# VectorE's products of a trace one piece ahead of its scans in a four-layer residual kernel

## What is computed

```python
ctx = causal_ema(x, tau_ctx)
wg = sigmoid(concat([x, ctx]) @ Wg.T + bg)
gated = x * wg
h1 = gelu(x @ Wn1.T + bn1)
mod = 0.5 + sigmoid(h1 @ Wn2.T + bn2)                 # one factor per token and trace
traces = [causal_ema(gated * mod[..., d], tau_raws[d]) for d in range(16)]
temporal = sum_d traces[d] * softmax(blend)[d]
gate = sigmoid(temporal @ Wtemp.T + btemp)
soma = gelu(x @ Wsoma.T + bsoma)
x = x + layernorm((soma * gate) @ Wout.T) * gamma + beta
x = x + pooled_attention(x)                           # second layer
x = x + mixture_of_9_experts(x)                       # third layer: 8 experts and a shared one
x = x + two_layer_head(x, expert_index)               # fourth layer
```

## Time and profile before

| | us |
|---|---|
| median of 3 runs (2808.72 to 2808.73) | 2808.72 |
| span of the profiled execution, first to last instruction | 2807.6 |
| TensorE busy | 2770.3 |
| VectorE busy | 1796.9 |
| ScalarE busy | 1449.7 |
| GpSimd busy | 1218.6 |
| mean granted TensorE clock | 0.998 |

### The profile page before, as it was taken

How to read it: one execution, slowest core, us unless ns; L and a number is a source line. 1 busy time by engine, 2 the same in 40 slices (tenths; PEclk the granted TensorE clock), 3 DMA queues, 4 the chain that set the end, 5 groups by cost and what they waited for, 6 DMA issues and landing times.

```text
span 2807.6 us, 36696 instructions
## 1 busy us (share of the span) xinstructions
PE 2770.3 (99%) x12794; PEld 2299.4 (82%) x12794; DVE 1796.9 (64%) x2976; ACT 1449.7 (52%) x2625; POOL 1218.6 (43%) x950
## 2 busy tenths in 40 slices
PE   8799999999999999999999999999999999999999
PEld 5678888888888888888888888888888888888888
DVE  8799778867777666556765766555766563333443
ACT  4555666566456544555545644455644563333445
POOL 5256435633554355434543345433454333333334
PEclk9999999999999999999999999999999999999999
DMA  4244333433223322112321222211322131111221
GB/s 154 81 145 125 100 105 104 145 98 102 77 68 99 107 68 68 57 59 69 104 64 59 82 87 74 68 47 57 111 80 66 42 103 45 46 45 46 79 89 58
DMA packets 117383, 230.37 MB, mean 82 GB/s; under 512 B 13672, under 2 KB 58960, under 8 KB 117200
## 3 DMA queue, kind: packets, MB, share of 16 engines
q1 hardware_dynamic: 81808, 190.15, 22.1%
q10 hardware_dynamic: 32832, 29.49, 4.2%
q0 software_dynamic: 2560, 8.39, 1.0%
HBM read 219.89 MB, written 8.09 MB: 81 GB/s over the span
## 4 chain that ended last, share of the span: by engine, by line
PE 93%; DVE 4%; issue 1%; ACT 1%; DMA 0%; SPq 0%; DVEq 0%; ACTq 0%
PE bank L588 20%; PE bank L589 20%; PE bank L590 20%; PE ps_out L588 10%; PE ps_out L590 10%; PE ps_out L589 10%; PE bank L581 1%; DVE trace L1130 1%; DVE trace L1138 1%; DVE w_lo L1210 1%; DVE hid L1244 0%; PE ps_out L581 0%; DMA pre_x<-in_xT 0%; PE bank L709 0%; PE bank L700 0%
## 5 line engine op out<-in xcount | busy, mean ns | idle before, releaser
L1383 POOL TENSOR_TENSOR hid_lo<-hid,hid_hi 128x512 fp32r<-128x512 f32 x640 | 851.0, 1330 | 1532.3 <-ACT hid_hi L1015 1532.0
L588 PE MATMUL bank<-res_lo,w_hi 128*128 128x512 f32 x2432 | 957.1, 394 | 5.7 <-DVE hid L1244 2.6
L589 PE MATMUL bank<-res_hi,w_lo 128*128 128x512 f32 x2432 | 948.6, 390 | 0.0
L590 PE MATMUL bank<-res_hi,w_hi 128*128 128x512 f32 x2432 | 947.4, 390 | 0.0
L1244 DVE TENSOR_TENSOR hid<-hid,bank 128x512 f32<-128x512 f32 x576 | 394.1, 684 | 623.5 <-PE bank L590 597.9
L984 ACT ACTIVATE hid<-bank 128x512 f32<-128x512 f32 x576 | 343.9, 597 | 589.0 <-PE bank L590 588.0
L1210 DVE TENSOR_TENSOR w_lo<-w_raw,w_hi 128x768 fp32r<-128x768 f32 (+2 forms) x520 | 495.0, 954 | 194.3 <-ACT w_hi L946 152.1
L946 ACT ACTIVATE w_hi<-w_raw 128x768 fp32r<-128x768 f32 x392 | 331.3, 845 | 480.5 <-PE ps_out L590 468.5
L588 PEld LDWEIGHTS bank<-res_lo,w_hi 128*128 128x128 f32 x2432 | 457.2, 188 | 99.0 <-issue 4.6
L590 PEld LDWEIGHTS bank<-res_hi,w_hi 128*128 128x128 f32 x2432 | 457.0, 188 | 96.9
L589 PEld LDWEIGHTS bank<-res_hi,w_lo 128*128 128x128 f32 x2432 | 457.4, 188 | 89.7
(11 more groups left out here) (180 smaller groups left out, 1565.4 us busy)
## 6 DMA issues: line engine op xcount, KB each, us to landing
w_raw<-in_chunks SPq DMA_DIRECT2D x392, 384.0 KB
mod_on<-mod_rows ACTq DMA_DIRECT2D x154, 128.0 KB
w_raw<-in_head_chunks SPq DMA_DIRECT2D x64, 224.0 KB
stat<-mod_rows ACTq DMA_DIRECT2D x70, 128.0 KB, 3.2
x_in<-in_xT SPq DMA_DIRECT2D x16, 256.0 KB, 3.8
pre_x<-in_xT SPq DMA_DIRECT2D x14, 256.0 KB, 7.3
soma_rows<-pre_soma SPq DMA_DIRECT2D x14, 256.0 KB, 2.0
soma<-soma_rows SPq DMA_DIRECT2D x14, 256.0 KB, 3.6
```

Of the source, the lines that this page charges most:

```text
L588: mm(out, wh, xl, start=start and i == 0, stop=False, skip_group_check=not lone)
L589: mm(out, wl, xh, start=False, stop=False, skip_group_check=not lone)
L590: last = mm(out, wh, xh, start=False, stop=end, skip_group_check=not lone)
L1383: nc.gpsimd.tensor_tensor(hid_lo[i % DEPTH][:], hid[i % 3][:], f(hid_hi[i % DEPTH][:]), ALU.subtract).then_inc(s_hlo, 1)
```

## The change

Piece 7 + d on VectorE now holds the product of trace d and then the scan of trace d-1; piece 7 holds only a product, and a new piece 23 only scan 15. GpSimd's addition of trace d moves from piece 8 + d to piece 9 + d; add 15 comes in piece 24, ahead of the gather. ScalarE's mix d waits for scan d-2 (mix 1: for mul 0) in place of scan d-1, which is the last VectorE work of the piece before in both versions. The product's wait for GpSimd begins at d = 3 in place of d = 4: mul 3 and mul 4 both wait for add 1, mul d for add d-3. The costs of pieces 7 and 23 change from 2.1 and 0.7 to 0.8 and 1.3, so the planner deals the pieces of blocks 1 to 7 anew.

```diff
--- before.py
+++ after.py
@@ -87,8 +87,8 @@
 
 def side_cost(b, j):
 
-    if 7 <= j < 7 + ND:
-        return 2.1
+    if 7 <= j <= 7 + ND:
+        return {7: 0.8, 7 + ND: 1.3}.get(j, 2.1)
     if b == 0 and j in (1, 26, 30, 32, 45):
         return 0.0
     return {0: 1.3, 5: 1.0, 34: 1.7, 36: 1.4, 42: 1.5, 24: 0.0, 25: 0.0, 29: 0.0, 37: 0.0, 43: 0.0}.get(j, 0.7)
@@ -267,7 +267,7 @@
 SIDE_ACT = (["x_hi", "ctx_hi", "h1", "soma", "mod", "gate", "alpha"] + [f"mix{d}" for d in range(ND)]
             + ["t_hi", "tgate", "p_hi", "sq", "q_hi", "cen", "std", "attn", "exp", "xT", "probT"])
 SIDE_DVE = (["ctx", "x_lo", "ctx_lo", "mod", "mod_hi", "modpair", "gated"]
-            + [f"{what}{d}" for d in range(ND) for what in ("mul", "scan")]
+            + [name for d in range(ND) for name in ([f"mul{d}", f"scan{d - 1}"] if d else ["mul0"])] + [f"scan{ND - 1}"]
             + ["t_lo", "prod", "p_lo", "q_lo", "rstd", "norm", "affine", "x1", "score",
                "max", "top", "xT_lo", "den", "rden", "prob", "probT_lo", "res"])
 SIDE_POOL = [f"add{d}" for d in range(1, ND)]
@@ -932,7 +932,7 @@
                     act.wait_ge(l_act[s], act_at(s, b, f"mix{d - 1}"))
                     if d + 2 < ND:
                         spread(s, b, d + 2)
-                    act.wait_ge(l_dve[s], dve_at(s, b, f"scan{d - 1}"))
+                    act.wait_ge(l_dve[s], dve_at(s, b, f"scan{d - 2}" if d > 1 else "mul0"))
                 act.wait_ge(s_on[s][k], 16 * ((ND // 3 + (k < ND % 3)) * (b - 1) + d // 3 + 1))
                 activate(ps_side[s][:, 0:S], mod_on[s][k][:], ACT.Copy, bias=1.0, scale=0.5).then_inc(l_act[s], 1)
 
@@ -1113,31 +1113,35 @@
                 elif j == 6:
                     dve.wait_ge(l_act[s], act_at(s, b, "gate"))
                     STT(gated[s][:], gated[s][:], 1.0, X[:], ALU.add, ALU.mult).then_inc(l_dve[s], 1)
-                elif 7 <= j < 7 + ND:
+                elif 7 <= j <= 7 + ND:
                     d = j - 7
-                    tr = trace[s][d % 3]
-                    if d == 0:
-                        mine("gated")
-                    if d == 0 and b == 0:
-                        done("blend")
-                    if d > 3:
-                        dve.wait_ge(l_pool[s], pool_at(s, b, f"add{d - 3}"))
-                    if b:
-                        dve.wait_ge(l_act[s], act_at(s, b, f"mix{d}"))
-                    else:
-                        dve.wait_ge(l_pe[s], pe_at(s, b, f"mix{d}"))
-                    for h in range(DH):
-                        last = STT(tr[:, h, :], gated[s][:, h, :], bl[:, h, d:d + 1],
-                                   (lead_mix[d % 2] if lead else ps)[:, 0:S], ALU.mult, ALU.mult)
-                    last.then_inc(l_dve[s], 1)
-                    mine(f"mul{d}")
-                    if d == 0 and b == 0:
-                        dve.wait_ge(l_act[0], act_at(0, b, "alpha"))
-                    decay = ps[:, S + d:S + d + 1] if b else lead_alpha[:, d:d + 1]
-                    for h in range(DH):
-                        last = V.tensor_tensor_scan((temporal[s] if d == 0 else tr)[:, h, :], decay.broadcast_to([P, S]),
-                                                    tr[:, h, :], 0.0, ALU.mult, ALU.add)
-                    last.then_inc(l_dve[s], 1)
+                    if d < ND:
+                        tr = trace[s][d % 3]
+                        if d == 0:
+                            mine("gated")
+                        if d == 0 and b == 0:
+                            done("blend")
+                        if d > 2:
+                            dve.wait_ge(l_pool[s], pool_at(s, b, f"add{max(d - 3, 1)}"))
+                        if b:
+                            dve.wait_ge(l_act[s], act_at(s, b, f"mix{d}"))
+                        else:
+                            dve.wait_ge(l_pe[s], pe_at(s, b, f"mix{d}"))
+                        for h in range(DH):
+                            last = STT(tr[:, h, :], gated[s][:, h, :], bl[:, h, d:d + 1],
+                                       (lead_mix[d % 2] if lead else ps)[:, 0:S], ALU.mult, ALU.mult)
+                        last.then_inc(l_dve[s], 1)
+                    if d:
+                        d -= 1
+                        tr = trace[s][d % 3]
+                        mine(f"mul{d}")
+                        if d == 0 and b == 0:
+                            dve.wait_ge(l_act[0], act_at(0, b, "alpha"))
+                        decay = ps[:, S + d:S + d + 1] if b else lead_alpha[:, d:d + 1]
+                        for h in range(DH):
+                            last = V.tensor_tensor_scan((temporal[s] if d == 0 else tr)[:, h, :], decay.broadcast_to([P, S]),
+                                                        tr[:, h, :], 0.0, ALU.mult, ALU.add)
+                        last.then_inc(l_dve[s], 1)
                 elif j == 26 and b:
                     dve.wait_ge(l_act[s], act_at(s, b, "t_hi"))
                     TT(one_lo[s][:], temporal[s][:], f(one_hi[s][:]), ALU.subtract).then_inc(l_dve[s], 1)
@@ -1362,7 +1366,7 @@
 
             def side(b, s, j):
                 if j == 24:
-
+                    add(b, s, ND - 1)
                     if b == 0:
                         done("onehot")
                     pool.wait_ge(l_pool[s], pool_at(s, b, f"add{ND - 1}"))
@@ -1370,13 +1374,15 @@
                     nc.gpsimd.indirect_dma_start(
                         out=trace[s][2][:].rearrange("p j l -> p (j l)"), out_offset=None, in_=penalties[:],
                         in_offset=bass.IndirectOffsetOnAxis(ap=pen_row[:, q:q + 1], axis=0)).then_inc(s_pen[s], 16)
-                elif 9 <= j < 8 + ND:
-                    d = j - 8
-                    pool.wait_ge(l_dve[s], dve_at(s, b, f"scan{d}"))
-                    if d > 1:
-                        pool.wait_ge(l_pool[s], pool_at(s, b, f"add{d - 1}"))
-                    nc.gpsimd.tensor_tensor(temporal[s][:], temporal[s][:], trace[s][d % 3][:],
-                                            ALU.add).then_inc(l_pool[s], 1)
+                elif 10 <= j < 9 + ND:
+                    add(b, s, j - 9)
+
+            def add(b, s, d):
+                pool.wait_ge(l_dve[s], dve_at(s, b, f"scan{d}"))
+                if d > 1:
+                    pool.wait_ge(l_pool[s], pool_at(s, b, f"add{d - 1}"))
+                nc.gpsimd.tensor_tensor(temporal[s][:], temporal[s][:], trace[s][d % 3][:],
+                                        ALU.add).then_inc(l_pool[s], 1)
 
             def late(i):
                 pool.wait_ge(s_hhi, i + 1)
```

## The result

The changed kernel takes **2831.96 us** (median of 4 runs, 2831.83 to 2833.25) against 2808.72 (4 runs, 2808.72 to 2812.88): ratio 1.0078, 95% interval 1.0066 to 1.0091. It is slower by 23 us, and the prediction, 2807.9 with a range up to 2816.0, missed it. The profiled execution took 2831.83 with a span of 2829.7; 2.1 us lie around the span, not 1.1 as I had assumed. The span grew by 22.1.

The account below looks back on a forecast made before the run. The prediction took TensorE, busy 99%, to bound the kernel. Lead -2.4, block 1's first lane +1.6 and the rest 0 summed to -0.8: span 2806.8, time 2807.9 us, range 2801.5 to 2816.

Parts of the forecast that it names:

- Base: Whole kernel: forecast summed on the profiled span of 2807.6 us, with 1.1 us added for the time around it.
- Lead, term 1: Block 0: scans no longer wait for the product just ahead, saving 0.12 us a trace over 29 pairs, -3.5 us.
- rival that the wait costs nothing: Block 0's traces: leaving out the wait gains nothing, so term 1 is 0 and the time 2811.4 us; chance 0.13.
- Lead, term 2: Block 0: product 3 newly waits for add 1 on GpSimd, starting at about 25.3 instead of 23.9 us, +1.4.
- the second wait: Block 0: a later product waits for GpSimd once, after lane 0's last addition and its penalty gather, 0.1 to 0.2 us.
- Block 1's first lane: 118 to 171 us: product 3's stall and more pieces before the next hids delay TensorE, +1.6 us, between 0 and +3.5.
- The rest: After 171 us: product 3's stalls are absorbed and TensorE's 12.0 us of idle stay, +-4, so 0 us.
- Product 3 reaching TensorE: Blocks after block 0: product 3's stalls delay TensorE, +10.3 us in all, time 2819.0; chance 0.15.
- That of no effect: Whole kernel: lead gain and lead stall cancel and block 1 is as before, time 2808.7 us; chance 0.08.
- The closings' idle: Closings of runs: shorter, newly dealt pieces remove half of TensorE's 12.0 us idle, time 2801.9 or 2800.3; chance 0.17.

Follow-up runs that it names:

- e9: e6 with each scan waiting for the product directly ahead of it instead of its own, same instructions and order: 2810.58 us.
- e2: The changed kernel with product 3 waiting for scan 0 on VectorE instead of add 1 on GpSimd: 2825.79 us.
- e1: The changed kernel with add 15 back in piece 23, the rest as changed: 2818.92 us.
- e7: The changed kernel with add 15 in piece 23 and product 3 waiting for scan 0, new costs kept: 2811.47 us.
- e5: The kernel before with the new order in block 0 only, product 3 not waiting for GpSimd, old costs: 2807.7 us.
- e6: The changed kernel with old costs, add 15 in piece 23 and product 3 waiting for scan 0: 2805.66 us.
- e8: The kernel before with only add 15 moved into piece 24, old order and old costs: 2818.36 us.
- e3: The kernel before with only the planner's new costs of pieces 7 and 23: 2818.26 us.

## Why the prediction was wrong, point by point

**Base.** Span plus 1.1 should have been span plus 2.1 for the changed kernel; that is 1 us of the 24 by which the forecast missed. (On the later chips the same difference is 1.8 for the kernel before.)

**Lead, term 1 (-3.5).** Right in cadence. VectorE in the changed kernel:

```profile
43.85 0.85 DVE L1131 SCALAR_TENSOR_TENSOR trace<-gated,bl,bank 128x256 f32<-128x256 f32 x2
44.62 1.26 DVE L1142 TENSOR_TENSOR_SCAN trace<-bank,trace 128x256 f32<-128x256 f32 x2
45.80 0.85 DVE L1131 SCALAR_TENSOR_TENSOR trace<-gated,bl,bank 128x256 f32<-128x256 f32 x2
```

1.95 us a trace, where the earlier trace rows had 2.07. The rival that the wait costs nothing is refuted for these two instructions by e9. The Trainium skill (VectorE: DVE Perf Modes, "The DRAIN you can't avoid") says that the flush is paid whether or not a semaphore follows and that the semaphore costs nothing extra; 2.07 against 1.94 us for the same instructions in the same order does not agree with that for this pair.

**Lead, term 2 (+1.4).** The wait is where and as long as forecast:

```profile
21.36 0.87 DVE L1131 SCALAR_TENSOR_TENSOR trace<-gated,bl,bank 128x256 f32<-128x256 f32 x2 [2.38 <-PE bank L661]
...
23.49 1.27 POOL L1384 TENSOR_TENSOR temporal<-temporal,trace 128x512 f32<-128x512 f32 x1 [2.32 <-DVE trace L1142]
24.80 0.87 DVE L1131 SCALAR_TENSOR_TENSOR trace<-gated,bl,bank 128x256 f32<-128x256 f32 x2 [1.39 <-POOL temporal L1384]
```

Its price was right too. From the third product's start to prod of lane 0 the changed kernel takes 63.84 us and e2, which lacks this wait alone, 62.51: 1.33. With add 15 early it is 64.23 in e1 and 62.93 in e7: 1.30. What was mis-sized is the second wait, forecast at 0.1 to 0.2 and 0.96 in the changed kernel:

```profile
79.14 0.87 DVE L1131 SCALAR_TENSOR_TENSOR trace<-gated,bl,bank 128x256 f32<-128x256 f32 x2 [0.96 <-POOL temporal L1384]
...
85.19 0.67 DVE L1152 SCALAR_TENSOR_TENSOR trace<-trace,soma 128x512 f32<-128x512 f32 x1
```

Lead in sum: prod 2.2 us earlier than in the earlier trace rows, the first hid 2.0, forecast 2.4. **Right**, with some luck: from the third product to prod VectorE gained only 1.8 (65.62 before, 63.84 now), and the third product itself came 0.4 earlier, which is scatter more than order: it starts at 21.46 to 22.08 in the three traces of the old order and at 21.03 to 21.93 in the nine of the new one. My own mark for it, the first expert matmul at 115.9 instead of 118.3, failed in this trace, 117.93, for another reason: TensorE's clock. It ran at its half level for longer behind the traces than in the kernel before; by 5 us (same columns as the windows above), the changed kernel:

```profile
101.00:106.00 5.00, 3.11 (x10) 2.01 (x10) 4.12 (x10) 2.67 (x7) 0.00 (x0) 0.65 0.14 33
106.00:111.00 5.00, 4.38 (x14) 3.70 (x15) 3.13 (x9) 2.06 (x6) 0.00 (x0) 0.50 0.41 128
...
116.00:121.00 5.00, 3.07 (x14) 2.57 (x15) 1.69 (x3) 2.04 (x4) 0.00 (x0) 1.00 0.00 0
```

and the kernel before:

```profile
106.00:111.00 5.00, 3.23 (x13) 2.41 (x14) 4.12 (x11) 4.10 (x12) 0.00 (x0) 0.79 0.27 81
...
116.00:121.00 5.00, 2.74 (x9) 2.21 (x9) 1.98 (x3) 1.10 (x3) 0.00 (x0) 0.81 0.00 0
```

0.50 is 1.2 GHz, 1.00 is 2.4 GHz; in the 5 us in which it fell TensorE was busy 3.11, in the 5 before (97.5 to 102.5) 2.91. Behind the first expert matmul the kernel before had its own slow stretch and the changed one had none, so by the first hid the gain was back. In e5, e6 and e7 that matmul came at 115.53, 115.75 and 115.92.

**Block 1's first lane (+1.6, between 0 and +3.5).** Right in size, in part by luck: -2.0 at the 1st hid, +0.1 at the 15th, +2.1. Product 3's stall, forecast at 4.7 us:

```profile
152.18 1.30 POOL L1384 TENSOR_TENSOR temporal<-temporal,trace 128x512 f32<-128x512 f32 x1
153.51 0.87 DVE L1131 SCALAR_TENSOR_TENSOR trace<-gated,bl,bank 128x256 f32<-128x256 f32 x2 [4.38 <-POOL temporal L1384]
...
163.81 0.60 PE L588 MATMUL bank<-res_lo,w_hi 128*128 128x512 f32 x1 [1.88 <-DVE hid L1248]
```

4.38 us. The addition ran 2.9 us earlier than I had placed it, and TensorE's wait came at 163.81, for hid, not at 171. In sum TensorE waited no longer between the two hids than before (1.9 and 0.6 us now; 0.7, 1.1 and 0.6 before). The clock is what differs. The changed kernel:

```profile
163.00:168.00 5.00, 4.20 (x12) 3.31 (x12) 5.00 (x8) 2.57 (x5) 3.67 (x3) 0.66 0.46 145
```

and the kernel before:

```profile
162.00:167.00 5.00, 3.86 (x17) 2.91 (x16) 5.00 (x5) 1.90 (x4) 2.83 (x3) 1.00 0.59 191
```

0.34 of 5 us is 1.7 us, most of the 2.1, and the prediction had no such term. The wait of product 3 is behind it all the same: in e2, which lacks it, TensorE waits 1.59 us there, the clock stays at 1.00, and the 15th hid is at -2.6.

**The rest (12.0 us of idle stay, +-4): the step that failed**, by 22.0 us on the ruler. It failed in three places, whose sizes are the rungs of the ladder read in the ruler's last column (-0.4, 5.7, 8.5, 22.0). (1) I costed the move of add 15 into piece 24 for the lead alone, where eight matmuls hide it, and never followed it in blocks 1 to 7: 13.5 us by e1 (22.0 - 8.5; both traces have one slow stretch of the clock, so it is not in the difference), 7.8 alone by e8. The diff and the planner's zero costs for pieces 24 and 25 both stood in the front part. (2) "Which pieces fall at a closing is dealt anew by the changed costs; the 12.0 us of idle stay the same in my forecast, +-4": the new deal alone costs 7.0 (e3), 6.1 on top of the rest (e7 less e6, 5.7 + 0.4); about 3 of the first and 1.6 of the second are slow stretches of the clock. (3) Product 3's stalls are not all absorbed: behind the 15th hid 2.8 (e1 less e7: the waits that e2 lacks at 964 and 1360 us, 1.5 and 1.0 on the ruler), and 3.3 up to there, where the clock's fall of 163 to 168 us is in it. The costs were not additive; the lane 0 stalls need the late add 15 and the new deal together. Product 3's wait with the old deal and add 15 early was not run by itself.

**The rivals.** Product 3 reaching TensorE had the right sign and of all the nearest time (2819.0). Its own price, 6.7 + 6.0 = 12.7 in the forecast, is about 7 by e2 and by e1 less e7, and it wasn't the mechanism that mattered most. The rival of the free wait is out by e9. That of no effect is out by the cadence of 1.95 us and by e5, though e5's 3 us are little. The closings' idle did not go: waits for acc rose from 4.5 to 6.7 us. (4.5 of the 12.0 us is 38%, not nearly half.)

**The range.** The one bound that had to be wide was that of the rest, and +-4 had no row behind it. Moving the releases of 14 chains by one step, at 2.0 us each, would have been a rival at +28 before any run.

## What to carry to other kernels

When a step moves to a later piece, follow its result to the next reader on every engine, in each stage and not only where the change was aimed: here an addition of 1.3 us, moved by one piece, stood behind another instruction in GpSimd's queue, and the matmul three handovers later stood on the critical path. Costs in a planner are part of the change; try them alone (e3 changed one rule of costs and found a third of the loss). A reordering aimed at one stage can be tried in that stage alone (e5) before the long body pays for it. And read the granted clock beside every difference of a microsecond or two between two traces.
